# Decoder layer on one core: q and k projected with the head dimension on the partitions, halves exchanged by transfers

## The reference

```python
q = (x @ Wq).reshape(b, l, H, HD).transpose(0, 2, 1, 3)      # H = 16, HD = 64
k = (x @ Wk).reshape(b, l, KV, HD).transpose(0, 2, 1, 3)     # KV = 4
v = (x @ Wv).reshape(b, l, KV, HD).transpose(0, 2, 1, 3)
q = q * cos + _rotate_half(q) * sin
k = k * cos + _rotate_half(k) * sin
attn = jnp.einsum('bhqd,bhkd->bhqk', q, k) / math.sqrt(HD)
attn = attn + slopes[None, :, None, None] * rel[None, None, :, :]
attn = jax.nn.softmax(attn, axis=-1)
out = jnp.einsum('bhqk,bhkd->bhqd', attn, v)
```

## Time and profile before

| | |
|---|---|
| median of 3 runs | 2226.62 us (2226.34 to 2226.76) |
| profiled execution, first to last instruction (span) | 2226.0 us |
| PE busy | 2139.8 us, 96% |
| PEld busy | 1665.6 us, 75% |
| DVE busy | 1955.4 us, 88% |
| ACT busy | 1699.3 us, 76% |
| POOL busy | 1421.1 us, 64% |
| DMA, all queues | 74.69 MB, mean 34 GB/s |
| mean granted TensorE clock | 0.995 of full |

### The profile page before, as it was taken

One profiled execution on the slowest core, in us unless ns is written; L12 is line 12 of the kernel. 1 busy time (PEld: TensorE's weight loads), 2 busy tenths in 40 slices (PEclk: granted clock), 3 DMA queues, 4 the chain that ended last, 5 costly groups with the idle time before them and its releaser, 6 DMA issues. The chain is left out here.

```text
span 2226.0 us, 58622 instructions
## 1 busy us (share of the span) xinstructions
PE 2139.8 (96%) x19659; PEld 1665.6 (75%) x19722; DVE 1955.4 (88%) x7980; ACT 1699.3 (76%) x4746; POOL 1421.1 (64%) x1670
## 2 busy tenths in 40 slices
PE   7899999999999999999999999999999999999986
PEld 5677777777777777777777777777777777777754
...
DMA packets 85401, 74.69 MB, mean 34 GB/s; under 512 B 18545, under 2 KB 79345, under 8 KB 85105
## 3 DMA queue, kind: packets, MB, share of 16 engines
...
## 5 line engine op out<-in xcount | busy, mean ns | idle before, releaser
L1467 POOL TENSOR_TENSOR prob<-prob,precs 128x512 f32<-128x512 f32 x512 | 528.9, 1041 | 560.9 <-DVE precs L1048 558.5
L1375 ACT ACTIVATE prob<-prob,nmax 128x256 f32<-128x256 f32 x1024 | 508.8, 504 | 45.3 <-DVE nmax L1041 45.3
L1041 DVE CUSTOM_DVE_ANT_0 prob<-bank,alibi 128x256 f32<-128x256 f32 x1024 | 371.4, 419 | 23.2 <-PE bank L755 22.8
L1382 ACT COPY pT<-bank 128x512 f32<-128x512 f32 x512 | 303.0, 592 | 56.8 <-PE bank L643 55.6
L643 PE MATMUL bank<-ident,prob 128*128 128x128 f32 x2048 | 316.2, 277 | 4.0 <-ACT pT L1382 3.3
L1399 ACT ACTIVATE px<-px,nmx 128x128 f32<-128x128 f32 x1024 | 313.8, 398 | 6.2 <-DVE nmx L1153 6.1
L643 PEld LDWEIGHTS bank<-ident,prob 128*128 128x128 f32 x2048 | 231.0, 141 | 55.9 <-issue 39.0
L774 PE MATMUL bank<-pT,v_sb 128*64 128x256 f32 x2048 | 250.9, 387 | 3.4 <-DVE qq_lo L1032 3.1
L1153 DVE CUSTOM_DVE_ANT_0 px<-bank,mask 128x128 f32<-128x128 f32 x1024 | 226.3, 286 | 2.5 <-issue 1.9
L774 PEld LDWEIGHTS bank<-pT,v_sb 128*64 128x64 f32 x2048 | 136.9, 137 | 101.3 <-issue 39.2
L1375 ACT ACTIVATION_READ_ACCUMULATOR prob<-prob,nmax 128x1 f32 x1024 | 198.9, 194 | 0.0
...
## 6 DMA issues: line engine op xcount, KB each, us to landing
...
kx<-k_sin SPq DMA_DIRECT2D x256, 32.0 KB, 2.0
...
```

Source lines behind the costliest of these rows:

```text
L1041: v.tensor_tensor_reduce(out=prob[:, (2 * p + q) % SLOTS, c, :], in0=psum[SCORES[c]][:, q * L:(q + 1) * L], in1=alibi[:, p % 2, :], scale= ...
L1375: nc.scalar.activation(prob[:, (2 * p + q) % SLOTS, c, :], prob[:, (2 * p + q) % SLOTS, c, :], ACT.Exp, bias=nmax[:, i:i + 1], scale=-1.0, ...
L1382: nc.scalar.copy(pT[:, p % 2, :, :, q * P:(q + 1) * P].rearrange("p c k n -> p (c k) n"), bank[:].rearrange("p (c n) -> p c n", c=4)).then ...
L1467: g.tensor_tensor(prob[:, n % SLOTS, :, :], prob[:, n % SLOTS, :, :], precs[:, 2 * n:2 * n + 2].unsqueeze(2).to_broadcast([P, 2, L]), ALU. ...
```

## The change

The projections of q and k are made with the weights stationary and the tokens moving, so that the head dimension lies on the partitions at once. There are five units per batch, in the order q pair 0, k, q pair 1, 2, 3 (`UNITS`, `GROUP`). The steps K, Q, kT and qT are gone. Per unit there are now:

- `proj` on PE: 12 matmuls of 256 columns into bank 3,
- `flat` on ACT: a scaled copy of the bank to SBUF, in one of two buffers,
- `swap` on SP: four transfers that exchange the blocks of 32 partitions of `flat` into `swap`,
- `turn` on DVE: `turn` = `flat` x cos, in one of three buffers; `turn` on POOL: `swap` x sin in place, then `turn` + `swap`,
- `part` on ACT: the high part; `part` on DVE: the rest.

The table `rope` is laid out with the head dimension on the partitions, `q_scale` is gone, bank 4 serves only O and W, and all tables `HEAD`, `BODY` and `TAIL` are new. The count of `fill` matmuls is the same, but in the last batch most of those that stood between the last steps stand behind the last one. The program also sets `dynamic_dma_scratch_size=1024`. The core of the diff:

```diff
-BANKS = dict(K=3, V=3, Q=3, kT=4, qT=4, O=4, W=4, T=2, TX=3, G=5, U=6, NX=7, QX=7, QXT=7, KV=7, KXT=7, OX=7, BX=7,
+BANKS = dict(proj=3, V=3, O=4, W=4, T=2, TX=3, G=5, U=6, NX=7, QX=7, QXT=7, KV=7, KXT=7, OX=7, BX=7,
...
+UNITS = 5
+GROUP = {0: 0, 2: 1, 3: 2, 4: 3}
...
+                    elif kind == "swap":
+
+                        n, = args
+                        i = (UNITS * b + n) % 2
+                        sp.wait_ge(*at("raw_ready", b, n))
+                        sp.wait_ge(*at("rot_sum", b, n - 2))
+                        for r in range(4):
+                            sp.dma_start(swap[r * 32:(r + 1) * 32, i, :, :], flat[(r ^ 1) * 32:(r ^ 1) * 32 + 32, i, :, :])\
+                                .then_inc(swapped[i], 16)
...
-                    elif kind == "K":
+                    elif kind == "proj":
+
+                        n, = args
                         pe.wait_ge(*at("x_lo", b))
                         pe.wait_ge(*freed(sem, bank, steps, place))
-                        for t in range(TT):
-                            last = project(0, t, psum[bank][:, t * 256:(t + 1) * 256], slice(0, 256))
+                        parts = ((x_hi, w_hi), (x_lo, w_hi), (x_hi, w_lo))
+                        for m in range(2):
+                            first = (m if n == 1 else 4 + 2 * GROUP[n] + m) * P
+                            for i in range(KT * 3):
+                                k, (xs, ws) = i // 3, parts[i % 3]
+                                last = mm(psum[bank][:, m * L:(m + 1) * L], ws[:, k, first:first + P], xs[:, k, :], start=i == 0, stop=i == KT * 3 - 1)
...
-                            pe.wait_ge(*at("k_ready", b))
+                            pe.wait_ge(*at("part_lo", b, 1))
                         if m == 0:
-                            pe.wait_ge(*at("q_ready", b, u))
+                            pe.wait_ge(*at("part_lo", b, u + 1 if u > 0 else 0))
...
+                    elif kind == "turn":
+                        n, = args
+                        i, j = (UNITS * b + n) % 2, (UNITS * b + n) % 3
+                        dve.wait_ge(*at("raw_ready", b, n))
+                        dve.wait_ge(*at("part_lo", b, n - 3))
+                        v.tensor_tensor(turn[:, j, :, :], flat[:, i, :, :], rope[:, 0:1, :].to_broadcast([P, 2, L]), ALU.mult)\
+                            .then_inc(sem["rot_cos"], 1)
+                    elif kind == "part":
+                        n, = args
+                        j = (UNITS * b + n) % 3
+                        hi, lo = (kk_hi[:], kk_lo[:]) if n == 1 else (qq_hi[:, GROUP[n] % 2, :, :], qq_lo[:, GROUP[n] % 2, :, :])
+                        dve.wait_ge(*at("part_hi", b, n))
+                        v.tensor_tensor(lo, turn[:, j, :, :], hi.bitcast(F32), ALU.subtract).then_inc(sem["part_lo"], 1)
...
+                    elif kind == "flat":
+                        n, = args
+                        i = (UNITS * b + n) % 2
                         act.wait_ge(*at("proj_mm", b, n))
-                        nc.scalar.copy(qtok[:, t, :], bank[:]).then_inc(sem["q_raw"], 1)
+                        act.wait_ge(*unit_swapped(b, n - 2))
+                        act.wait_ge(*at("rot_cos", b, n - 2))
+                        nc.scalar.activation(flat[:, i, :, :], psum[home(b, "proj", n)][:].rearrange("p (m n) -> p m n", m=2), ACT.Copy,
+                                             scale=1.0 if n == 1 else 0.125 / FACTOR[GROUP[n]]).then_inc(sem["raw_ready"], 1)
+                    elif kind == "part":
+                        n, = args
+                        j = (UNITS * b + n) % 3
+                        hi = kk_hi[:] if n == 1 else qq_hi[:, GROUP[n] % 2, :, :]
+                        act.wait_ge(*at("rot_sum", b, n))
+                        act.wait_ge(*at("S_mm", b, 2 * GROUP[n] - 3 if n != 1 else -1))
+                        nc.scalar.copy(hi, turn[:, j, :, :]).then_inc(sem["part_hi"], 1)
...
+                    elif kind == "turn":
+                        n, = args
+                        i, j = (UNITS * b + n) % 2, (UNITS * b + n) % 3
+                        pool.wait_ge(*unit_swapped(b, n))
+                        g.tensor_tensor(swap[:, i, :, :], swap[:, i, :, :], rope[:, 1:2, :].to_broadcast([P, 2, L]), ALU.mult).then_inc(sem["rot_sin"], 1)
+                        pool.wait_ge(*at("rot_sin", b, n))
+                        pool.wait_ge(*at("rot_cos", b, n))
+                        g.tensor_tensor(turn[:, j, :, :], turn[:, j, :, :], swap[:, i, :, :], ALU.add).then_inc(sem["rot_sum"], 1)
```

156 lines of the change are left out of this document (51 added, 105 removed), and 396 rows, old and new, of tables (BODY, HEAD, TAIL).

## The result

The changed kernel takes 2331.59 us (median of 4 runs, 2330.03 to 2332.15), the kernel before beside it 2226.69 (2226.34 to 2227.57): a ratio of 1.0472, interval 1.0459 to 1.0485. It is 105 us slower, where 55 us faster was forecast. The profiled execution took 2331.39 us, its span is 2329.6.

A forecast was written before the change was run, and what follows sets the result against it. TensorE's in-order stream was taken as the bound, 65.69 us per batch. Less 2.57 for transposes, plus 0.8 of idle time gives 63.92; 31 x 1.77 = 55 off 2226.6 makes 2172 us, range 2143 to 2222.

The forecast's parts named there:

- TensorE's part: PE stream per batch: five transpose steps leave, 2.57 us; turned projections cost nought, bounds -0.2 and +0.5; 65.69 to 63.12 us.
- ScalarE stayed hidden: ACT's copies and high parts: +0.4 to +0.9 us on 52.5 us per batch, near 84% busy, off the path.
- The transfers stayed hidden: Twenty more 64 KB swap transfers per batch on SyncE, costed at nothing, with 14 us left for queues.
- The block: VectorE's ten new operations with two SBUF inputs stand still behind GpSimd: 2.1 us per batch, DVE at 60.9 us.
- the random estimate: Wait of VectorE's new operations behind GpSimd at random arrivals: 0.4 us each, 4 us per batch; half was taken.
- the places ahead of a reciprocal: Seven of ten new VectorE operations stand shortly before a reciprocal GpSimd often waits for, so the 4 us was halved.
- The third rival: VectorE's new operations each wait 0.65 us, GpSimd is pushed back, prob tiles late to the transposes: 2276 us, 12%.
- point of decision: The slower case, with VectorE and GpSimd stopping each other, decides from 0.49 us of wait per new VectorE operation.
- What is late next: With PE at 63.12 and DVE at 60.9 us, PE's idle time grows by 0.8 us per batch: period 63.92.
- The head: Start of the run: the chain through transposes becomes one of about equal length with a transfer, within 3 us, left out.
- The tail: End of the run: dummy matmuls (L713) move behind the last step; small clock cost, left out of the sum.
- the two terms named: At the end of the run: up to 3 us of clock cost, less 1 us the dummy matmuls themselves took.

The follow-up runs named there:

- e5: Changed kernel without its swap transfers from batch 4 on, GpSimd reading rope in place of swap and waiting for flat alone: 2334.16 us, ratio 1.048.
- e2: Changed kernel with only HC (hq from hh on VectorE) replaced from batch 4 on by a tensor_reduce over 512 elements: 2276.99 us, ratio 1.0231.
- e3: Changed kernel with VectorE's ten turn and part operations per batch and HC replaced by tensor_reduces from batch 4 on: 2243.65 us, ratio 1.0077.
- e4: Kernel before, own order, with eleven VectorE rotation operations reading two SBUF tensors instead of PSUM and one from batch 4 on: 2287.32 us, ratio 1.0272.
- e13: Changed kernel with one entry of VectorE's BODY table moved, HS 1 five places forward: 2290.38 us, ratio 1.029.
- e8: Changed kernel with all its work and the HEAD, BODY and TAIL tables rearranged: 2197.64 us, ratio 0.9871 against the kernel before.
- e14: Changed kernel with HEAD, BODY and TAIL rearranged, plus 38 dummy matmuls at each of two gaps of the head: 2195.02 us, ratio 0.986.

## Why the prediction was wrong, point by point

**TensorE's part was right.** The transposes that left were worth 2.59 us per batch (forecast 2.57), the projections with V, in their new form, 9.15 to 9.23 for 9.18 (a change of nought was forecast, bounds -0.2 and +0.5). Weight loads cost nothing, as the rows of both forms had said. ScalarE stayed hidden. The transfers stayed hidden (e5), at the DMA share of 0.19 that was named.

**The block: the size of its own part was right, its reach was not.** Half of the random estimate was taken, 2.1 us per batch for the ten operations. Measured: 5 x (0.944 - 0.693) + 4 x (0.854 - 0.693) + (1.244 - 0.693) = 1.3 + 0.6 + 0.6 = 2.5 us, 0.25 for each. Three things were left out of the step.
- HC. It reads and writes SBUF as L1240 does, and the new order moved it behind `turn` and beside GpSimd: (1612 - 684) x 2 = 1.9 us per batch, 55 us of the program (e2). The front part names HC as an operation with SBUF operands, and the step counted only the new ones.
- GpSimd's side. The same block stretches its ten operations by 5 x 0.17 + 5 x 0.12 us and `c_lo` by 0.44, 1.9 us for these eleven. Small ones stretched as well: `z_rstd` 718 to 1155 ns, `f_var` 216 to 555, `f_neg` 226 to 585, `y_var` 230 to 542, another 1.4 us. All are back in e3. Nothing of that stood in the sum, which held that GpSimd's idle time would cover its extra work.
- The path. The step asked whether DVE would become full. It did not (91.9%). What counts is that prob's chain crosses both engines, DVE's reciprocal and GpSimd's product, before TensorE's transposes, and a stop of either is at once a stop of TensorE where the distance in the order is short. Its weight loads wait 2.8 us per batch for prob alone.

Waits of 2.5 + 1.9 = 4.4 us on VectorE and 3.3 on GpSimd have thus made the period 3.1 us longer (68.43 - 65.31).

The argument that the places ahead of a reciprocal protect the new operations was weak. It supposes that GpSimd waits for precs there; at 1053.55, in the timeline above, it has `hh` to do instead.

The Trainium skill ("SBUF — State Buffer", section "SBUF: two separate sides") names two kinds of VectorE instruction that take the exclusive lock against GpSimd: those with two SBUF inputs, and those in a two-port mode. The runs agree on the first: `by_sin` takes 887 ns for 686 when its inputs move to SBUF (e4). The prediction applied the rule to the ten new operations alone. HC would fit the second kind: it handles 1024 elements in 684 ns, where an addition of 512 takes 693. No run shows the mode as such.

**The third rival came closest.** It had the mechanism, each engine pushed back in turn and prob late to the transposes, at 2276 us and 12%. Its point of decision was wrong. It put it at 0.49 us of wait for each operation, from the room left on DVE; the operations waited 0.25, and the kernel lost 2.7 us per batch.

**"What is late next" failed.** TensorE's idle time was to grow by 0.8 us. With every block taken away (e3) the period is 65.31, not 63.12 + 0.8 = 63.92: 2.2 us over the pure stream of 63.1, 1.4 more than said. It is the order: `hs` 5 us late to GpSimd, prob products behind it and 1.4 us of waits for prob left on TensorE, px transposes up by 1.66 us. With HS 1 moved (e13) the wait for prob falls to 0.4 us. How the 2.2 us divide among the places of the order is not settled. This could have been read ahead of the run: the two tables side by side show HS 1 behind R 13 on VectorE, and on GpSimd the `hh` of HS 1 ahead of prob products. With the tables rearranged the period is 64.05 us (e8), 0.13 from the forecast, but the time is 2197.64, 26 us above it: the 31 batches gain 42.7 us where 55 were forecast, and the head loses 10.3. So the forecast period was that of a good order for this change, not of the one that came with it, and the forecast time was not reached by any.

**The head failed.** Within 3 us was said, 19.2 was measured. The series of weight preparations ahead of the first scores, blocked `px` operations (1.52 for 0.41) and 24 us at 1.2 GHz were all outside the argument, which looked only at the chain of the first unit. The clock can explain only the smaller part: e8 has 24 us at 1.2 GHz too, by the same windows, and is 9 us shorter than the changed kernel up to the first `amx`; e14 has 7, and is 3 us shorter again, within the scatter. The cause of the rest stays open.

**The tail was right:** +1.3 us, within the two terms named.

**The sum with what was measured:** before 2226.0; transposes and projections, -2.54 x 31 = -79; waits of the new order by itself, (65.31 - 63.15) x 31 = +67; the block, 3.12 x 31 = +97; head +19, tail +1: 2331, where the span was 2329.6. By the first and last `amx` in place of the periods the first two terms are together -5.7 and the third is +88.8, and with +19.2 and +1.3 that gives 2329.6. The two ways differ by 8 us in the block's share, so that is known to some 10 us.
